# Cross attention: another order in three engines' lists, squares read from SBUF, and the keys' reciprocal root on GpSimd

## What is computed

```python
kvx = jnp.einsum('bsi,oi->bso', cond, w_kv_x)
kx, vx = jnp.split(kvx, 2, axis=-1)
kx = _ln(kx.reshape(b, sc, g, d), kxln_w, kxln_b)      # (x - mean) * rsqrt(var + 1e-5) * w + b, over d = 128
vx = vx.reshape(b, sc, g, d)
xout = _gqa(qx, kx, vx).reshape(b, s, nh * d)          # softmax(q k / sqrt(d)) v
```

## Time and profile before

| | us |
|---|---|
| median of 3 runs | 2798.78 (2798.61 to 2798.89) |
| profiled execution | 2799.96, its span 2798.2 |
| PE busy | 2278.0 (81%) |
| DVE busy | 2104.4 (75%) |
| GpSimd busy | 1571.4 (56%) |
| ACT busy | 1554.5 (56%) |

### The profile page before, as it was taken

The page is one execution under the profiler, slowest core; times in us unless marked ns, Lnnn a source line. Parts: engine busy times, 40 slices in busy tenths (PEclk is TensorE's granted clock), DMA queues, the critical chain, the costliest instruction groups (busy, mean ns, idle before and its releaser), DMA issues. The chain is left out here.

```text
span 2798.2 us, 50477 instructions
## 1 busy us (share of the span) xinstructions
PE 2278.0 (81%) x18514; PEld 1812.5 (65%) x18514; DVE 2104.4 (75%) x4502; ACT 1554.5 (56%) x3129; POOL 1571.4 (56%) x1619
## 2 busy tenths in 40 slices
PE   2466662699999999999999999999999999855556
PEld 1243441578877877877877877877877878644334
DVE  8888885477787778778787787778778787558763
ACT  4455451566666666666666666666666667411211
POOL 2465655766766766767666766766767655340000
PEclk8687875999999999999999999999999999977778
DMA  2001103110010010110110111010010100073100
GB/s 105 16 29 40 46 23 115 55 38 31 26 50 32 25 44 34 31 44 32 32 38 31 34 43 32 32 44 26 31 52 25 32 9 1 1 271 96 40 12 8
DMA packets 74482, 119.45 MB, mean 43 GB/s; under 512 B 21168, under 2 KB 56576, under 8 KB 73216
## 3 DMA queue, kind: packets, MB, share of 16 engines
q1 hardware_dynamic: 74240, 116.23, 12.3%
HBM read 94.20 MB, written 22.02 MB: 42 GB/s over the span
## 5 line engine op out<-in xcount | busy, mean ns | idle before, releaser
L71 PE MATMUL x_kc<-x_wk,x_ctxT 128*128 128x256 f16 x4992 | 622.8, 274 | 52.8 <-POOL x_ctxT L975 40.0
L997 POOL TENSOR_TENSOR x_kT<-x_kf,x_kT 128x512 f16<-128x512 f32 (+1 forms) x448 | 629.6, 1405 | 37.3
L71 PE MATMUL x_ox<-x_ctxp,x_pt 128*128 128x256 f16 x4992 | 619.0, 273 | 0.0
L995 POOL TENSOR_SCALAR x_kT<-x_kf 128x512 f16<-128x512 f32 (+1 forms) x448 | 288.2, 643 | 583.8 <-ACT x_kf L1067 581.8
L71 PEld LDWEIGHTS x_kc<-x_wk,x_ctxT 128*128 128x128 f16 x4992 | 481.6, 98 | 131.6 <-issue 40.2
L71 PEld LDWEIGHTS x_ox<-x_ctxp,x_pt 128*128 128x128 f16 x4992 | 486.3, 98 | 70.1 <-DVE x_on L1328 14.0
L1055 ACT ACTIVATE x_kraw<-x_kc 128x512 f32<-128x512 f32 (+1 forms) x448 | 254.3, 568 | 426.3 <-PE x_kc L71 214.5
L1263 DVE TENSOR_REDUCE x_ss<-x_sq 128x4 f32<-128x512 f32 (+1 forms) x448 | 283.1, 642 | 230.5 <-ACT x_sq L1059 228.9
L1320 DVE TENSOR_TENSOR x_pt<-x_tp,x_pt 128x512 f16<-128x512 f32 (+1 forms) x512 | 297.4, 584 | 117.5 <-ACT x_pt L1094 113.7
L1067 ACT ACTIVATE x_kf<-x_tp,x_hv 128x512 f32<-128x512 f32 (+1 forms) x448 | 330.7, 755 | 76.5 <-PE x_tp L1146 72.7
L1181 PE MATMUL x_tp<-x_ident,x_pb 128*128 128x128 f32 x1664 | 256.5, 274 | 52.8 <-ACT x_pb L1088 50.6
(11 more groups left out here) (234 smaller groups left out, 3181.5 us busy)
## 6 DMA issues: line engine op xcount, KB each, us to landing
x_stage<-in_ctxT SPq DMA_DIRECT2D x32, 800.5 KB, 4.3
x_stage<-in_ctx SPq DMA_DIRECT2D x16, 896.0 KB, 5.1
x_stage<-in_ctx SPq DMA_DIRECT2D x16, 640.0 KB
scr_q<-a_qxT SPq DMA_DIRECT2D x8, 1024.0 KB, 3.9
x_qs<-scr_q SPq DMA_DIRECT2D x16, 512.0 KB, 5.4
scr_core<-a_catc SPq DMA_DIRECT2D x8, 512.0 KB, 2.6
scr_x<-x_catx SPq DMA_DIRECT2D x8, 512.0 KB, 2.6
f_area<-in_wprojT SPq DMA_DIRECT2D x4, 1024.0 KB, 11.4
```

The costliest lines, as they stand in the source:

```text
L71: last = pe.matmul(out, lhs[i], rhs[j], start=start and n == 0, stop=stop and n == len(parts) - 1)
L995: gp.tensor_scalar(dst[0], src, 1.0, 0.0, ALU.mult, ALU.add).then_inc(khi_ready, 1)
L997: gp.tensor_tensor(dst[1], src, dst[0], ALU.subtract).then_inc(kT_ready, 1)
```

## The change

In PE's list (`ORDER`) the third product of the group before, `pv` -1 2, moves from between two turns of probabilities to a place ahead of `tr` 1; `m` 1 moves behind `ob`, and `tr` 2 ahead of `m` 2. In ACT's list `tr` 1 and `tr` 2 move ahead of `m` 1 and `m` 2. In DVE's list `ob` moves ahead of `m` 0, the division `on` -1 ahead of `pt` 0 2, and the `rs` entries go.

The square is read from `kraw` in SBUF. ACT waits for its own copy first, and PE's key product waits for the copy in place of the square.

The root is on GpSimd, behind the last split of keys of the step. GpSimd's version has 14 instructions in place of 11, since each step of the iteration takes three two-input instructions and one with two constants. In the set-up the first root comes after the conversions of context, the second after the first seven splits.

```diff
-        ORDER = [("m", 0), ("sr", 0), ("sc", 0), ("pv", -1, 0), ("pv", -1, 1), ("tr", 0), ("oa", -2), ("m", 1),
...
+        ORDER = [("m", 0), ("sr", 0), ("sc", 0), ("pv", -1, 0), ("pv", -1, 1), ("tr", 0), ("oa", -2), ("pv", -1, 2),
...
+            def root(JK):
+                gp.wait_ge(ss_ready, (JK + 1) * KU)
+                if not (isinstance(JK, int) and JK < 1):
+                    gp.wait_ge(kn_ready, JK * 2)
+                gp.tensor_scalar(ss[:], ss[:], 1.0 / D, EPS * WSCALE * WSCALE, ALU.mult, ALU.add).then_inc(k_chain, 1)
+                gp.wait_ge(k_chain, SETUP_K + JK * K_OPS + 1)
+                gp.tensor_scalar(rk[:].bitcast(I32), ss[:].bitcast(I32), -0.5, RSQRT_SEED, ALU.mult, ALU.add).then_inc(k_chain, 1)
+                for n in range(2, K_OPS):
+                    gp.wait_ge(k_chain, SETUP_K + JK * K_OPS + n)
+                    if n % 4 == 2:
+                        ins = gp.tensor_tensor(tk[:], rk[:], rk[:], ALU.mult)
+                    elif n % 4 == 3:
+                        ins = gp.tensor_tensor(tk[:], tk[:], ss[:], ALU.mult)
+                    elif n % 4 == 0:
+                        ins = gp.tensor_scalar(tk[:], tk[:], -0.5, 1.5, ALU.mult, ALU.add)
+                    else:
+                        ins = gp.tensor_tensor(rk[:], tk[:], rk[:], ALU.mult)
+                    ins.then_inc(k_chain, 1)
+
+            root(0)
             for i in range(KU):
                 split_unit(0, 0, i)
+            root(1)
...
+                    if exists(t, j, ("rs", 0)):
+                        root(JK + 1)
...
-                act.activation(sq[:, (jk * KU + i) % 2, 0:n], src, ACT.Square).then_inc(sq_ready, 1)
+                act.wait_ge(kraw_ready, 4 + u + 1)
+                act.activation(sq[:, (jk * KU + i) % 2, 0:n], kraw[:, 4 * i:4 * i + n // P, :].rearrange("p n d -> p (n d)"),
+                               ACT.Square).then_inc(sq_ready, 1)
...
-                    pe.wait_ge(sq_ready, u)
+                    pe.wait_ge(kraw_ready, 4 + u)
```

More of the change, by code:

```diff
@@ L798, in last @@
             return isinstance(t, int) and t == TILES - 1
-        ORDER = [("m", 0), ("sr", 0), ("sc", 0), ("pv", -1, 0), ("pv", -1, 1), ("tr", 0), ("oa", -2), ("m", 1),
[2 rows of a table removed]
+        ORDER = [("m", 0), ("sr", 0), ("sc", 0), ("pv", -1, 0), ("pv", -1, 1), ("tr", 0), ("oa", -2), ("pv", -1, 2),
[2 rows of a table added]
                  ("tr", 4), ("oa", -1), ("pv", 0, 1), ("m", 5), ("tr", 5), ("ob", -1), ("tr", 6), ("pv", 0, 2),
                  ("pt", 1, 0), ("m", 6), ("pt", 1, 1), ("pt", 1, 2), ("pv", 0, 3), ("pt", 1, 3)]
-        ACT_ORDER = [("sr", 0), ("m", 0), ("tr", 0), ("oa", -2), ("exp", 0), ("m", 1), ("tr", 1), ("pt", 0, 0),
[1 row of a table removed]
+        ACT_ORDER = [("sr", 0), ("m", 0), ("tr", 0), ("oa", -2), ("exp", 0), ("tr", 1), ("m", 1), ("pt", 0, 0),
[1 row of a table added]
                      ("m", 4), ("tr", 4), ("oa", -1), ("exp", 1), ("m", 5), ("tr", 5), ("tr", 6), ("pt", 1, 0),
                      ("m", 6), ("pt", 1, 1), ("pt", 1, 2), ("pt", 1, 3)]
-        DVE_ORDER = [("norm", 0), ("max", 0), ("oa", -2), ("norm", 1), ("m", 0), ("m", 1), ("ob", -2), ("quant", 0),
[1 row of a table removed]
+        DVE_ORDER = [("norm", 0), ("max", 0), ("oa", -2), ("norm", 1), ("ob", -2), ("m", 0), ("m", 1), ("quant", 0),
[1 row of a table added]
                      ("quant", 2), ("m", 3), ("max", 1), ("quant", 3), ("m", 4), ("oa", -1), ("m", 5), ("quant", 4),
[3 rows of a table removed]
[2 rows of a table added]
         TP_KINDS = ("sr", "tr", "pt", "oa", "ob")
@@ L877, in pieces @@
                     yield stage[:, half, lo:hi], [ctxT[:, slot, p, half, lo:hi] for p in range(2)]
+        SETUP_K = 4
+        K_OPS = 2 + 3 * 4
         block = ctx.enter_context(nc.Block("x_blk"))
@@ L1253, in _ @@
                                        ).then_inc(wk_ready, 1)
-            SETUP_K = 4
             v.wait_ge(ready, 32)
@@ L1264, in square_sum @@
                                 X, ALU.add).then_inc(ss_ready, 1)
[L1266 to L1284, removed]
             def normalise(JK, half):
@@ L1302, in part @@
                     normalise(J + 1, o[1])
-                elif kind == "rs":
-                    root(J + 2, o[1])
                 elif kind == "m":
@@ L1368, in _ @@
                     square_sum(JK, JK, i)
-                for n in range(K_OPS):
-                    root(JK, n)
                 if JK == 0:
```

## The result

The changed kernel takes 2922.4 us (median of 4 runs, 2920.5 to 2924.0) against 2798.8 for the kernel before on the same chip: a ratio of 1.0441, 95% interval 1.0423 to 1.0459. It is slower by 124 us. The forecast was slower, 2880 us, with 2795 to 2965 as its range; the time lies inside, 42 us above the value given.

What follows compares the result with a forecast made beforehand. POOL's last split of keys was taken to close each step. Root 1.2 plus middle 0.3 less 0.1 for DVE relief gave 1.4 us over 57 steps, 80, plus 5 for set-up and last steps: 2880 us, range 2795 to 2965.

Steps and rivals of the forecast that it cites:

- The bound: End of each step: POOL's last split of keys, ending 0.14 us ahead of PE's head product, closes the step.
- The root: 14 POOL instructions behind the last split take 4.6 us, so normalisation starts 1.7 us later, near 4.55 behind the head.
- The spare time: Between the normalised keys being ready and PE reaching the first key transpose: 0.5 us spare.
- PE's standstill: PE waits 1.2 us before the first key transpose for the late normalised keys.
- Third product ahead of the turn: At the first turn of probabilities, 1.31 us of product covers the 0.79 wait, but PE meets the gain again next.
- What is behind the turn: Middle of the step: squares and division cost 0.6 in three steps, the quantising step wins 0.7; mean loss 0.3 us.
- The 0.1 taken off for DVE's shorter list: End of the step: without the root on DVE, turned probabilities come some 0.5 earlier, worth 0 to 0.1 us.
- The root that fits: Rival, chance 0.16: POOL's root takes 3.4 us and hides behind PE's 4.66; 2816 us, or 2790.
- the far longer one: Rival, chance 0.12: POOL's root instructions average 0.55 us, the root takes 7.7; 3055 us.
- The faster rival: Rival, chance 0.12: root fits, division does not gate the middle, 0.79 a step returns at the turn; 2754 us.

Runs made afterwards that it cites:

- late_conv: orders_on with POOL's fourth conversion put behind the last split of keys and DVE's root instructions behind the turned pieces; 2738.8 us.
- orders_on: The kernel before with the new PE, ACT and DVE lists, division behind the third turned piece, root on DVE, squares from PSUM; 2754.1 us.
- on_ahead: The kernel before with all new lists as changed, division ahead of the third turned piece, root on DVE, squares from PSUM; 2813.0 us.
- root_back: The changed kernel with the root's eleven instructions back in their old places in DVE's list, new lists and SBUF squares kept; 2827.2 us.
- early0: The kernel before with the root in two parts on DVE, the first four units' root and first normalisation in the step's second half; 2908.6 us.
- early1: early0 with PE's first key transpose also put ahead of the scores, and ACT's list to match; 2895.8 us.
- the two misses: early0 and early1, the kernel before with the root in two parts on DVE; 2908.6 and 2895.8 us.
- root_it4: The changed kernel with a fourth iteration of the root, four more GpSimd instructions in each root; 3051.0 us.

## Why the prediction was right, and where its sum was short

**The bound: right.** POOL's last split ended 0.09 to 0.15 ahead of the head in every steady step of the changed kernel. late_conv adds that the next limit is near: with that end moved 0.7 forward, a step gains 0.25.

**The root: its length near, its price short.** The root was put at 4.6 us and took 4.31; twice the 2.4 of DVE's eleven instructions, the other size that the prediction names, would have been 0.5 too long. The normalisation was put at 4.55 behind the head, measured 48.88 - 44.56 = 4.32. The spare time is as read: the normalisation starts 1.50 later, the turn 1.03 (5.69 behind the head for 4.66), so 0.47 was spare. PE's standstill was put at 1.2; it is 0.88, and 1.03 against the kernel before. What the sum didn't contain is that the late root also costs behind the turn. That ACT's copy would be late too was said; that it then stands in front of the scaling, and that all of ACT's list moves with it, was not followed up. It is 0.3 a step with the squares from the banks: 62 x (1.03 + 0.3) = 82, where the three pairs of kernels give 77, 80 and 90. In the changed kernel it is 0.47, and the pair gives 95.

**Third product ahead of the turn: half right.** The wait of 0.79 is gone. That PE meets it again at the next place holds only with the division ahead of the piece; without it orders_on keeps 0.64 a step.

**What is behind the turn: the step that failed.** The sum took 0.3 us a step for it, from 0.6 in three steps and -0.7 in the one with the quantisation. Measured from the turn of keys, in the kind of step shown above, with one part of the change added from column to column:

| | before | predicted | lists (orders_on) | and division (on_ahead) | and squares (root_back) | and root (after) |
|---|---|---|---|---|---|---|
| third sum starts | 8.53 | 8.6 | 8.03 | 8.03 | 8.45 | 8.86 |
| middle head product | 10.44 | 11.0 | 9.81 | 10.71 | 10.75 | 11.24 |
| next head | 24.82 | 25.4 | 24.18 | 25.09 | 25.36 | 25.83 |

Up to root_back the prediction's working comes out: 25.36 for 25.4, with the middle head product 0.25 sooner than it was put. (The division, to the next instruction, was put at 1.15 and took 1.04.) Two terms of the sum were wrong. First, the root was given no price behind the turn, and has 0.47 of it, 0.34 in the quantising step. Second, in the quantising step 0.7 was to be won, by POOL's shorter wait in front of its third split. That wait did go: 1.84 in the usual step to none, but 0.18, 1.96 and 0.36 came up in front of the fourth, fifth and sixth, 2.50 in all. In the quantising step POOL's waits behind the first split went from 1.53 to these rows:

```profile
1094.18 0.64 POOL L997 TENSOR_SCALAR x_kT<-x_kf 128x512 f16<-128x512 f32 x1 [0.39 <-ACT x_kf L1094]
1099.62 0.62 POOL L997 TENSOR_SCALAR x_kT<-x_kf 128x512 f16<-128x512 f32 x1 [1.74 <-ACT x_kf L1094]
1103.67 1.47 POOL L997 TENSOR_SCALAR x_kT<-x_kf 128x512 f16<-128x512 f32 x1 [1.06 <-ACT x_kf L1094]
```

The late middle head product moves the fifth and sixth turn of keys in this step as in the others. Instead of 0.7 won, 0.34 is lost there with the root on DVE and 0.68 in the changed kernel. Behind the turn, the four kinds of step grew by 1.02, 0.67, 1.03 and 1.01, 0.93 on average, in place of 0.3. 57 x (1.02 + 0.93) = 111, and some 12 us lie outside these steps, for 5 predicted; together 123 of the 124. That the forecast of 81 us more lies as near as it does owes something to luck: a standstill put 0.2 too long and the two missing terms partly cancel. The 0.1 taken off for DVE's shorter list has no run of its own.

**The rivals.** The root that fits needed 3.5 us and took 4.31; the far longer one needed 0.55 an instruction, and it was 0.31. The faster rival fell with the root; yet orders_on has its two conditions, no root on POOL and no division in the middle, and its 2754.1 is the 2754 that the rival gave. So near an agreement is chance: against the kernel beside it the gain is 47 and not 45.

**What lies outside the steady steps, and what stays open.** PE's first head comes 0.7 us later than before (534.00 for 533.27), which is the set-up; the first step takes 31.44 for 27.78, 3.7 more; and 8.1 lie behind the 57 steps, in the last six and the end. The last part is not explained further. Open is also why early0 is slower than early1: no run separates these.

## What to carry to other kernels

An engine with idle time isn't free if its idle time lies behind the instruction that closes the loop: the root went to POOL's 6.4 idle us, but could only start when POOL's last split, the loop's end, was done, and its reader had 0.5 us to spare. Price a moved chain by when its result is needed, and then follow everything else that waits for that result, for it is released at the same moment and queues up. In lists written by hand, a few small instructions ahead of a piece that the critical engine waits for can cost more than the rest of the edit gains: the new lists alone gained 45 us, and three small instructions in the wrong place took 59.

## What the runs showed of the hardware

**Narrow instructions on GpSimd are quick.** 26 columns take 0.22 us with one input and 0.23 to 0.24 with two, and follow each other, each waiting for the one before, in 0.30 to 0.33. Over the span 560 to 2430 us (count, busy us, mean ns):

```profile
L1013 POOL TENSOR_TENSOR x_tk<-x_tk,x_ss 128x26 f32<-128x26 f32 x177 | 42.7, 241 | 13.8
...
L1015 POOL TENSOR_SCALAR x_tk<-x_tk 128x26 f32<-128x26 f32 x177 | 38.9, 220 | 15.5
```

The two-input form costs a tenth more than the other at this width, and not the double that wide ones show (1.16 against 0.62).

**A small DVE instruction can last as long as a large one on GpSimd.** One of the root's instructions in early1, and POOL beside it:

```profile
1010.56 1.13 DVE L1270 SCALAR_TENSOR_TENSOR x_tk<-x_tk,x_ss 128x18 f32<-128x18 f32 x1
```

```profile
1010.50 1.16 POOL L984 TENSOR_TENSOR x_kT<-x_kf,x_kT 128x512 f16<-128x512 f32 x1
```

DVE's instruction ends at 1011.69, POOL's at 1011.66: it had waited for POOL's end. So had, by the same signs, the first instruction of the division in the kernel before, whose 0.94 the prediction could only bound: it ends at 1026.88, and so does POOL's subtraction that began at 1025.72 and lasted 1.16. It is likely also a cause of the two misses: the last instruction of an iteration takes 0.19 on average at the end of the step and 0.62 amid POOL's splits. No run shows how much of the misses that is. The other way round, POOL's first subtraction of a step, beside DVE's multiply of 2304 columns, takes 3.34 in place of 1.16, in the kernel before (from 1017.99) as in the changed one (from 1053.11): both kernels pay these 2.2 us on POOL in each step. The Trainium skill (SBUF — State Buffer, "Who interferes with whom") says that a VectorE instruction with two inputs in SBUF and a GpSimd instruction that reads SBUF exclude each other for the whole instruction; the two ends, 0.03 us apart, agree.

**TensorE's clock fell behind a wait of 2.08 us,** from 2.4 to 1.2 GHz, in 49 steps of root_it4, and stayed full behind the same wait in nine others; behind the waits of 0.88 in the changed kernel it did not fall.
